# Second attention: ScalarE copies the scores out of their banks first

## The reference

```python
scores = einsum('bqhd,bkhd->bhqk', q, k) / sqrt(16)   # 154 scores per token and head
top_s, top_i = top_k(scores, 16)
attn = softmax(top_s)
o = einsum('bhqk,bhqkd->bqhd', attn, v gathered at top_i)
```

## Time and profile before

| | |
|---|---|
| median of 3 runs | 1472.02 us (1468.61 to 1472.67) |
| profiled execution | 1467.48 us |
| its span | 1465.7 us |
| TensorE busy | 1359.6 us, 93% of the span |
| VectorE | 901.9 us, 62% |
| ScalarE | 726.0 us, 50% |
| GpSimd | 346.1 us, 24% |

### The profile page before, as it was taken

How to read it: one execution, slowest core, us unless ns; L and a number is a source line. 1 busy time by engine, 2 the same in 40 slices (tenths; PEclk the granted TensorE clock), 3 DMA queues, 4 the chain that set the end, 5 groups by cost and what they waited for, 6 DMA issues and landing times.

```text
span 1465.7 us, 25433 instructions
## 1 busy us (share of the span) xinstructions
PE 1359.6 (93%) x9100; PEld 681.3 (46%) x9100; DVE 901.9 (62%) x2785; ACT 726.0 (50%) x1484; POOL 346.1 (24%) x397
## 2 busy tenths in 40 slices
PE   7989887889999888999899999999999989989998
PEld 5457654444644653442233333343333335545676
DVE  3656579988888896765565666666676346640220
ACT  2245456665485564035544565555556664543221
POOL 1013257876666664010000100000010011010220
PEclk9999989889999999999999999999999999999999
DMA  6011003000000000000010000000000000000000
GB/s 196 21 56 34 17 19 107 2 15 1 1 2 12 30 2 28 1 1 1 1 52 21 1 2 0 2 1 1 1 12 1 2 1 2 13 6 0 15 19 29
DMA packets 22093, 26.75 MB, mean 18 GB/s; under 512 B 4204, under 2 KB 19634, under 8 KB 21708
## 3 DMA queue, kind: packets, MB, share of 16 engines
q1 hardware_dynamic: 21059, 25.03, 5.3%
q10 hardware_dynamic: 909, 0.10, 0.1%
HBM read 21.58 MB, written 3.08 MB: 17 GB/s over the span
## 4 chain that ended last, share of the span: by engine, by line
PE 78%; DVE 11%; ACT 4%; issue 4%; POOL 1%; DMA 1%; SPq 0%; ACTq 0%; DVEq 0%; POOLq 0%
PE bank L1098 27%; PE bank L1056 11%; PE bank L1138 8%; PE bank L1070 7%; PE bank L1035 5%; PE bank L1014 4%; PE bank L993 2%; PE bank L1162 2%; PE bank L1041 2%; DVE left L1581 2%; PE bank L1181 1%; DVE x_hat L1526 1%; DVE top L1578 1%; DVE left L1588 1%; PE bank L1021 1%
## 5 line engine op out<-in xcount | busy, mean ns | idle before, releaser
L1337 ACT ACTIVATE pr<-bank 128x512 f32<-128x512 f32 x656 | 353.4, 598 | 283.6 <-PE bank L1098 270.3
L1553 DVE TENSOR_REDUCE part_max<-bank 128x1 f32<-128x512 f32 x512 | 327.2, 685 | 178.5 <-PE bank L1098 178.0
L1098 PE MATMUL bank<-slot 32*128 32x512 f32 (+1 forms) x3072 | 388.2, 522 | 10.8 <-ACT pr L1337 6.1
L1098 PEld LDWEIGHTS bank<-slot 32*128 32x128 f32 x3072 | 162.6, 187 | 209.5 <-issue 157.8
L1605 POOL TENSOR_SCALAR var_eps<-mean_var 128x4 f32<-128x4 f32 x24 | 5.5, 229 | 882.5 <-DVE mean_var L1517 882.0
L1664 POOL TENSOR_SCALAR left<-left 128x308 f32<-128x308 f32 x128 | 125.3, 979 | 76.0 <-issue 34.3
L1138 PE MATMUL bank<-pr,v 128*17 128x512 f32 x1024 | 135.2, 600 | 0.2
L1056 PE MATMUL bank<-h_t,w_m 128*128 128x512 f32 x256 | 127.9, 625 | 4.3 <-DVE o_all L1497 3.2
L1666 POOL TENSOR_TENSOR probs<-left,exp_all 128x308 f32<-128x308 f32 x128 | 107.5, 840 | 10.7
L1359 ACT ACTIVATE exp_all<-bank,neg 128x154 f32<-128x154 f32 x256 | 85.6, 386 | 6.6 <-DVE left L1581 2.1
L1578 DVE MAX8 top<-bank 128x8 f32<-128x154 f32 x256 | 69.5, 313 | 30.6 <-PE bank L1162 30.0
(11 more groups left out here) (142 smaller groups left out, 1757.0 us busy)
## 6 DMA issues: line engine op xcount, KB each, us to landing
w_m<-in_L_xcond_w_m SPq DMA_DIRECT2D x1, 2048.0 KB, 7.9
w_m<-in_L_xcond_w_m SPq DMA_DIRECT2D x2, 1024.0 KB, 7.9
w<-in_L_xcond_w SPq DMA_DIRECT2D x2, 1024.0 KB, 6.6
w_ada<-in_L_xcond_w_ada SPq DMA_DIRECT2D x1, 1792.0 KB, 10.1
x_sb<-in_x SPq DMA_DIRECT2D x6, 256.0 KB, 6.3
res_row<-rows_dram SPq DMA_DIRECT2D x12, 128.0 KB, 3.4
out_x<-x_sb SPq DMA_DIRECT2D x6, 256.0 KB, 2.1
wa<-in_L_xcond_w_qkv SPq DMA_DIRECT2D x1, 768.0 KB, 6.6
```

What stands on the lines that cost most here:

```text
L1098: last = nc.tensor.matmul(g.bank(*tile)[:, into], left, right, start=True, stop=True)
L1337: nc.scalar.activation(m.pr[:, u % NPR, :], g.bank("s", gi, i)[:, :], ACT.Exp).then_inc(g.free("s", gi, i), 1)
L1553: nc.vector.tensor_reduce(m.part_max[:, slot, h * TB + i // 8, i // 4 % 2:i // 4 % 2 + 1], bank[:, :], axis=AX.X, op=ALU.max).then_inc(don ...
```

## The change

A new step c_lift on ScalarE copies a half's scores (308 of the bank's columns) into one of three places m.lift in SBUF. c_top and c_exp_all read the copy. A bank of scores is free when its lift is done. The scores are planned 1.3 steps ahead instead of 0.8 (from unit 2 on), the lift 0.9 steps ahead of c_top (0.2, 0.2, 0.35 and 0.8 in units 0 to 3). A lift waits for left1 and the exps of three halves before, which read the same place. Lift 0 waits for the end of the first attention (group 7), and c_top of unit 0 is no longer planned 9 us early.

```diff
--- before.py
+++ after.py
@@ -145,7 +145,7 @@
 SOON = ("ck_a", "cv_copy", "x_hat", "on_copy", "modulate", "ua_copy", "silu", "qk_a", "v_copy")
 LATE = ("ck_d", "x_sum", "stats", "rstd", "hid", "qk_d", "out_sum")
 FOLLOW_UPS = {"v": "v_copy", "ua": "ua_copy", "ub": "hid", "ug": "gelu", "on_turn": "on_copy", "y_mm": "x_sum", "hat_turn": "modulate",
-           "o_turn": "o_norm", "m": "m_red", "m_turn": "m_copy", "s": "exp", "c_score": "c_exp_all", "c_turn": "c_copy",
+           "o_turn": "o_norm", "m": "m_red", "m_turn": "m_copy", "s": "exp", "c_score": "c_lift", "c_turn": "c_copy",
            "cv": "cv_copy", "ctx_turn": "ctx_copy", "mcol": "mcol_add", "mgate": "mgate_add", "mbv": "mres", "mtp": "mtp_add"}
 
 
@@ -478,10 +478,11 @@
                 for t in range(4 * half, 4 * half + 4):
                     t0 = start + u * step
                     sooner = (9.0, 4.0)[u] if u < 2 else 0.0
-                    plan.at(t0 - 0.8 * step - sooner, ("c_score", gi, t, 0), ("c_score", gi, t, 1), ("c_scores", gi, t))
+                    plan.at(t0 - (0.8 if u < 2 else 1.3) * step - sooner, ("c_score", gi, t, 0), ("c_score", gi, t, 1), ("c_scores", gi, t))
                     for hf in range(2):
                         t1 = t0 + 0.5 * hf * step
-                        plan.at(t1 - (sooner if u == 0 else 0.0), ("c_top", gi, t, hf))
+                        plan.at(t1 - (0.2, 0.2, 0.35, 0.8, 0.9)[min(u, 4)] * step, ("c_lift", gi, t, hf))
+                        plan.at(t1, ("c_top", gi, t, hf))
                         plan.at(t1 + 0.12 * step, ("c_neg", gi, t, hf))
                         plan.at(t1 + 0.25 * step, ("c_exp_all", gi, t, hf))
                         plan.at(t1 + 0.55 * step, ("c_pick", gi, t, hf))
@@ -723,6 +724,7 @@
     m.left2 = scratch("left2", [P, 4, 2, S2])
     m.top = scratch("top", [P, 4, 2, TOPK])
     m.exp_all = scratch("exp_all", [P, 4, 2, S2])
+    m.lift = scratch("lift", [P, 3, 2, S2])
     m.probs = scratch("probs", [P, 2, HG, P + HW])
     m.tails_t = scratch("tails_t", [P, 512])
     m.probs_t = nc.alloc_sbuf_tensor_at("probs_t", [P, HG, 512], F32, offset=place["v1"])
@@ -735,6 +737,7 @@
     m.rows_dram = nc.dram_tensor("rows_dram", (B, 9, C), F32).ap()
     sem = lambda name: ctx.enter_context(nc.semaphore(name))
 
+    m.lifted = sem("lifted")
     m.p_mm, m.free = sem("p_mm"), [sem(f"free{i}") for i in range(7)]
     m.m_mm, m.s_mm, m.c_mm, m.turned, m.pv_done = (sem(n) for n in ("m_mm", "s_mm", "c_mm", "turned", "pv_done"))
 
@@ -800,7 +803,7 @@
             return []
         if before[0] == "c_score":
             v = self.plan.order[before]
-            return [(self.m.left1_done, 2 * v + 2), (self.m.all_done, v + 1)]
+            return [(self.m.lifted, v + 1)]
         return [self.freed(*before)]
 
     def ran(self, *step):
@@ -1342,6 +1345,15 @@
             if i >= 2:
                 act.wait_ge(*g.ran("o_turn", *g.o_order[i - 2]))
             nc.scalar.activation(m.o_st[:, i % 2, :], m.bank[7][:, :], ACT.Copy).then_inc(m.o_copied, 1)
+        elif kind == "c_lift":
+            v = plan.order[step]
+            act.wait_ge(m.c_mm, v + 1)
+            if v == 0:
+                act.wait_ge(*g.group_end(7))
+            since(act, (m.left1_done, 2 * (v - 2)))
+            since(act, (m.all_done, v - 2))
+            bank = g.bank("c_score", *step[1:])[:, :].rearrange("p (h c) -> p h c", h=2)
+            nc.scalar.activation(m.lift[:, v % 3, :, :], bank[:, :, 0:S2], ACT.Copy).then_inc(m.lifted, 1)
         elif kind == "c_neg":
             v = plan.order[step]
             act.wait_ge(m.picked, 4 * v + 2)
@@ -1354,9 +1366,8 @@
             if v == 0:
                 act.wait_ge(*g.group_end(7))
             since(act, (m.pick_done, v - 3))
-            bank = g.bank("c_score", *step[1:])
             for hh in range(2):
-                last = nc.scalar.activation(m.exp_all[:, v % 4, hh, :], bank[:, hh * C:hh * C + S2], ACT.Exp, bias=m.neg2[:, v % 4, hh:hh + 1])
+                last = nc.scalar.activation(m.exp_all[:, v % 4, hh, :], m.lift[:, v % 3, hh, :], ACT.Exp, bias=m.neg2[:, v % 4, hh:hh + 1])
             last.then_inc(m.all_done, 1)
         elif kind == "c_copy":
             _, gi, t = step
@@ -1569,16 +1580,15 @@
             nc.vector.tensor_copy(m.max_sb[:, i % 2, :], g.bank("m_turn", gi)[0:HG * TB, 0:P]).then_inc(g.free("m_turn", gi), 1)
         elif kind == "c_top":
             v = plan.order[step]
-            bank = g.bank("c_score", *step[1:])
-            dve.wait_ge(m.c_mm, v + 1)
+            dve.wait_ge(m.lifted, v + 1)
             if v == 0:
                 dve.wait_ge(*g.group_end(5))
             since(dve, (m.neg_done, v - 3))
             for hh in range(2):
-                nc.vector.max(m.top[:, v % 4, hh, 0:8], bank[:, hh * C:hh * C + S2]).then_inc(m.picked, 1)
+                nc.vector.max(m.top[:, v % 4, hh, 0:8], m.lift[:, v % 3, hh, :]).then_inc(m.picked, 1)
             for hh in range(2):
                 dve.wait_ge(m.picked, 4 * v + hh + 1)
-                nc.vector.match_replace(m.left1[:, v % 2, hh, :], m.top[:, v % 4, hh, 0:8], bank[:, hh * C:hh * C + S2], -FAR).then_inc(m.left1_done, 1)
+                nc.vector.match_replace(m.left1[:, v % 2, hh, :], m.top[:, v % 4, hh, 0:8], m.lift[:, v % 3, hh, :], -FAR).then_inc(m.left1_done, 1)
             for hh in range(2):
                 dve.wait_ge(m.left1_done, 2 * v + hh + 1)
                 nc.vector.max(m.top[:, v % 4, hh, 8:16], m.left1[:, v % 2, hh, :]).then_inc(m.picked, 1)
```

## The result

The changed kernel takes 1484.95 us (median of three executions; a fourth, slow one took 3190.84 and is left out) against 1470.43 for the kernel before on the same chip (median of four): a ratio of 1.0104, 95% interval 1.0083 to 1.0124. It is slower by 15 us; 1466 was forecast, with a range up to 1481. The executions that were profiled, 1482.07 and 1467.48 us, both lie some 3 us under these medians, so the 14.6 us between their spans are nearly the whole loss.

The account below looks back on a forecast made before the run. TensorE was busy 93% of the span, but in the second attention no engine was full and the bound changed. Terms −4.1 + 2.6 − 1.0 − 2.5 − 3.4 + 2.0 = −6.4 us gave about 1466 from 1472.0, range 1453 to 1481.

Parts of the forecast that it names:

- Banks come free earlier: Second attention: scores wait only for the lift, so TensorE's 8.2 us wait for exps goes; half taken, −4.1 us.
- The row that was to inherit: TensorE's 9.4 us wait for GpSimd's selection (L1173), to which part of the removed wait for exps would move.
- The start: Start of second attention: lift 0 waits for the first attention's last pv, so half 2 starts later; +2.0 us.
- The lifts: 128 ScalarE copies and dearer exps, hidden by ScalarE's waits except in four silu bursts, half hidden there; +2.6 us.
- The upper end of +62: Upper end of the lifts' term: all 54.7 us of copies and 7.7 us of exps standing on the path.
- VectorE's wait moves: VectorE's 30.0 us wait for scores partly becomes a wait for lifts; half of TensorE's 5.0 us stops saved, −2.5 us.
- clock −3.4: Two TensorE stops are each followed by a lowered granted clock, 3.4 us lost each; one of two goes, −3.4 us.
- VectorE reads the copy: VectorE's MAX and replace read SBUF, 6 ns quicker each, 3.1 us in all; a third counts, −1.0 us.
- ScalarE as the bound: Rival: ScalarE fills in the two MLP windows, delaying hidden copies and exps; +8.8 us, 1481 us, chance 0.17.
- The changed name of the wait: Rival: VectorE's 30.0 us wait for scores becomes a wait on the lift; −0.5 us, 1471.5 us, chance 0.28.
- forecast 11.0: The predicted gains together: banks −4.1, reading the copy −1.0, VectorE's wait −2.5, clock −3.4 us.

Follow-up runs that it names:

- e1: Kernel before with only the scores planned 1.3 steps ahead instead of 0.8, no copies: 1526.84 us, ratio 1.0385.
- e8: Kernel before with the late start alone (unit 0's selection not planned early, half 0 waiting for group 7), no copies: 1473.77 us, ratio 1.0025.
- e10: Changed kernel with copy leads 0.2, 0.45 and 0.9 from unit 2 on, late start kept: 1473.83 us, ratio 1.0036 to the kernel before.
- e2: Kernel before plus 128 unread ScalarE copies of 308 elements from a constant tile at the lifts' queue places: 1482.33 us, ratio 1.0083.
- e7: Changed kernel with copies in kt's place and early start, each copy from half 3 on made twice, second unread: 1497.25 us, ratio 1.0183.
- e6: Changed kernel with copies in kt's place and early start, scores 0.8 and copies 0.45 steps ahead: 1495.58 us, ratio 1.0193.
- e5: Changed kernel with early start and six copy places, scores 2.4 and copies 1.9 steps ahead from unit 6: 1470.01 us, ratio 1.0006.
- e12: Changed kernel with only unit 2's copy lead changed, 0.65 steps instead of 0.35, banks unchanged: 1481.04 us, ratio 1.0077 to the kernel before.

## Why the prediction was wrong

**Banks come free earlier (−4.1): the mechanism held.** The 8.2 us are gone, and e1 shows what this order costs without the copies. What the gain is in the time was not measured by itself. The row that was to inherit (GpSimd's probabilities, 9.4 us) stands at 10.1; a second heir was not seen, TensorE's wait for probs_t, from 1.6 to 11.6.

**The start (+2.0) failed first.** The late start itself was sized right: counted from the end of the first attention half 2 comes 2.2 us later, and e8 has +1.6 at half 8 and +3.7 in the whole. The sentence "the scores of unit 2, which want o_norm's bank, are late by as much" holds too: they start 5.8 us behind that end, 3.6 before. But what stands behind these scores was put at nothing. c_turn of unit 0 follows them and the scores of unit 3, c_copy follows c_turn, half 5's copy follows c_copy in ScalarE's queue: c_copy is 4.7 us later, MAX stands 4.19 us, and the loss is 6.9 us at half 8 instead of 2. The clock is not the difference, it reads 0.83 over 185 to 215 in both kernels. e10 gives back 10 us without touching the late start. The prediction took the leads of units 0 to 3 from the diff and never laid ScalarE's queue out for these units; the order c_turn, c_copy, lift that it did lay out for the steady state is at its worst there, at a lead of 0.35.

**The lifts (+2.6) failed second.** 54.1 us of copies and 8.6 more of exps are the work that was forecast. But hiding was judged by busy time: bursts of 20.4 in 20 us, 1.3 us each, half hidden. One of the two windows was also misread: 400 to 420 holds x_hat and no silu; the silus of the second block of tokens stand in 429 to 449, where ScalarE was busier still before, and those of the first came 9 us later in the changed kernel (first line before, second line changed):

```profile
429.00:449.00 20.00, 17.87 (x95) 8.30 (x94) 14.38 (x80) 18.98 (x36) 11.62 (x13) 1.00 0.07 20
330.00:350.00 20.00, 17.89 (x99) 8.53 (x98) 11.40 (x62) 18.43 (x36) 12.71 (x14) 1.00 0.09 27
```

The engine was not at 20 there and yet VectorE stood 2.9 to 4.0 us at each burst, since a copy behind a table load and two silus waits for all of them, however free ScalarE is on average. Off the bursts too it is not free: e2 puts the work alone at 12 us, e7 at 0.4 us a us. The upper end of +62 was stated, the value taken near the low end.

**VectorE's wait moves (−2.5, clock −3.4): no.** It was to shrink below 30.0 and became 43.2. The chain c_turn, c_copy, lift was seen and weighed right in kind; that it would be longer than the one with the filler in it was not. e6 to e5 show what decides it, the leads of scores and copies in the queues. TensorE's two stops behind VectorE did go (3.1 and 1.9 us are 0.5 and 0.4), but others came, and its waits for VectorE in the stage went from 6.6 to 9.6 us. The granted clock over the stage went from 0.94 to 0.92, so the clock gave nothing back.

**VectorE reads the copy (−1.0): sized right.** MAX 313 to 308, replace 308 to 303. By the Trainium skill (VectorE: DVE Perf Modes, the TRN2 errata) a bank as source would cost VectorE 62 cycles more, an estimate of 65 ns at 0.96 GHz. The two rows differ by 5. The same table has ScalarE the other way round, dearer from SBUF by 52 cycles, an estimate of 43 ns at 1.2 GHz; the exps agree in sign, 386 to 416 ns.

Of the rivals, ScalarE as the bound (1481) had the right side and the right engine, but not the place: its MLP windows did not fill, and TensorE waits for hidden copies 3.1 us. That its number lies 4 us from the measured one is luck. The changed name of the wait is what the wait row shows, without its forecast of no change.

The account by the ratios: late start +3.7 (e8), queue place at the start +4, bank at the start (or the leads of units 1 and 3) +6 (e12, e10); that leaves (1.0036 − 1.0025) × 1470 = 1.6 of the 15.3, the difference of the lifts' cost (12 by e2) and of all gains. So the gains together would be about 10 us, near the forecast 11.0. This sum takes the parts as independent and is worked out, not measured; the one part without a run of its own is the gain of free banks with the copies at no cost. The traces agree in kind and not in size: at half 8 they have 1.6 for the late start (2.1 with e10), 2.0 for the place and 2.8 for the bank, and from half 16 to half 127 the changed kernel loses 3.7 us where e2 loses 11.8. How the loss divides between these parts stays open to some us.

## What to carry to other kernels

When a copy on a half-idle engine is put between two others, don't ask how busy that engine is: lay out its queue around each copy and look for the longest thing that stands in front of it (here a silu with its table load, and a step that waits for TensorE), and give the copy a lead longer than that. Lay out the first few units separately, where leads are short, places are late and banks are still held by what came before. If the engine must touch the data anyway, let that be its real work (the exp) and not a copy.

## What was not expected of the hardware

ScalarE's 308 elements took 423 ns from a bank and 459 ns from a constant SBUF tile read through a broadcast pattern (e2); which of the two, memory or pattern, makes the 36 ns was not tried.
